# Attention, routing and a three-of-sixteen mixture of experts on one core: the two sums are filled in the attention's turns, and TensorE gets unread products at two joints

## The reference, cut to what matters

```
x: (4, 1024, 256) f32
proj = x @ W_in.T + b_in                    # q, k, v: 16 heads of 64
q, k = rope(q), rope(k)
att  = softmax(causal(q @ k.T / 8))
x    = layernorm(x + (att @ v) @ W_out.T + b_out)
gates = softmax(x @ gate)                   # 16 experts
top 3 of the 16 per token, their gates scaled to a sum of 1
y    = sum over the 3 chosen e of gate_e * (relu(x @ W1[e] + b1[e]) @ W2[e] + b2[e])   # hidden 512
out  = layernorm(x + y)
```

## Time and profile before

| What | Value |
| --- | --- |
| median of 3 runs | 1839.72 us (1834.96 to 1841.53) |
| profiled execution, its own time | 1837.63 us |
| span of its trace | 1834.3 us |
| busy, share of the span | PE 92%, DVE 75%, POOL 67%, ACT 39% |
| attention | 0 to about 1284 us |
| routing | about 1285 to 1360 us |
| experts | about 1360 to 1794 us |
| last phase | about 1794 to 1834 us |

### The profile page before, as it was taken

The page is one execution under the profiler, slowest core; times in us unless marked ns, Lnnn a source line. Parts: engine busy times, 40 slices in busy tenths (PEclk is TensorE's granted clock), DMA queues, the critical chain, the costliest instruction groups (busy, mean ns, idle before and its releaser), DMA issues. The chain is left out here.

```text
span 1834.3 us, 34020 instructions
## 1 busy us (share of the span) xinstructions
PE 1686.4 (92%) x9515; PEld 1264.3 (69%) x9516; DVE 1383.9 (75%) x3235; ACT 722.0 (39%) x1519; POOL 1233.9 (67%) x1064
## 2 busy tenths in 40 slices
PE   4689999999999999999999999998659999999990
PEld 3556667666766677666766676664339999999980
DVE  3578888888888888988888898875776566656654
ACT  2234444444445544444444444543332222222222
POOL 3256788677877777788767787764017777777764
PEclk8799999999999999999999999999759999999995
DMA  9976556655665676456666565542974444444448
GB/s 307 336 207 162 154 168 199 182 164 157 184 163 156 209 205 179 140 160 187 199 188 187 166 188 142 161 127 98 355 241 72 71 73 74 71 73 74 71 65 278
DMA packets 185058, 302.36 MB, mean 165 GB/s; under 512 B 23120, under 2 KB 82384, under 8 KB 184800
## 3 DMA queue, kind: packets, MB, share of 16 engines
q1 hardware_dynamic: 161360, 269.20, 49.7%
q0 software_dynamic: 21504, 30.29, 10.4%
q10 hardware_dynamic: 2064, 1.31, 0.3%
HBM read 188.81 MB, written 111.67 MB: 164 GB/s over the span
## 5 line engine op out<-in xcount | busy, mean ns | idle before, releaser
L780 ACT ACTIVATE prob<-b_ps 128x512 f32<-128x512 f32 (+3 forms) x768 | 354.4, 488 | 360.3 <-PE b_ps L589 260.3
L516 POOL TENSOR_TENSOR acc<-acc,prob 128x1024 f32<-128x1024 f32 (+1 forms) x192 | 352.8, 1837 | 6.4 <-POOL acc L516 3.6
L588 PE MATMUL b_ps<-q,k 128*128 128x512 f32 (+3 forms) x768 | 296.1, 390 | 5.3 <-ACT prob L780 3.5
L489 POOL TENSOR_TENSOR roped<-rot 128x512 f32<-128x512 f32 x128 | 174.5, 1364 | 165.0 <-DVE rot L919 164.2
L581 PE MATMUL a_ps<-k,q 128*128 128x512 f32 (+3 forms) x768 | 265.8, 383 | 20.5 <-DMA k<-scratch_hilo 10.1
L670 PE MATMUL y_ps<-prob,v_sb 128*64 128x512 f32 (+3 forms) x1536 | 272.9, 490 | 0.1
L899 DVE CUSTOM_DVE_ANT_0 masked<-a_ps,causal 128x128 bf16<-128x128 f32 (+3 forms) x512 | 237.3, 479 | 45.9 <-PE a_ps L581 37.7
L589 PE MATMUL b_ps<-q,k 65*128 65x512 f32 (+3 forms) x768 | 264.4, 348 | 0.0
L1449 POOL DMA_INDIRECT scratch_sum<-y,dst_i x112 | 187.6, 1675 | 94.8 <-ACT y L1521 90.9
L948 DVE RECIPROCAL inv<-inv 128x128 f32<-128x128 f32 x256 | 232.2, 929 | 7.7 <-ACT inv L821 5.3
L494 POOL TENSOR_TENSOR lo<-roped,hi 128x512 fp32r<-128x512 f32 x128 | 176.8, 1382 | 80.6 <-ACT hi L793 80.6
(11 more groups left out here) (255 smaller groups left out, 2382.9 us busy)
## 6 DMA issues: line engine op xcount, KB each, us to landing
q<-scratch_hilo SPq DMA_DIRECT2D x192, 256.0 KB, 4.6
k<-scratch_hilo SPq DMA_DIRECT2D x192, 256.0 KB, 5.2
scratch_hilo<-hi SPq DMA_DIRECT2D x64, 512.0 KB, 3.8
scratch_hilo<-lo SPq DMA_DIRECT2D x64, 512.0 KB, 4.5
w_sb<-scratch_wsplit SPq DMA_DIRECT2D x32, 512.0 KB, 3.6
w<-in_L_ffn_W_dram SPq DMA_DIRECT2D x32, 512.0 KB, 9.9
wv_sb<-scratch_wsplit SPq DMA_DIRECT2D x16, 512.0 KB, 5.9
xT<-scratch_xsplit SPq DMA_DIRECT2D x6, 1024.0 KB, 6.2
```

The costliest lines, as they stand in the source:

```text
L516: nc.gpsimd.tensor_tensor(sums, old, probs(q), ALU.add).then_inc(m["sum_p"], 1)
L588: nc.tensor.matmul(out, k1[s][:, h, js], q1[s][:, h, qs], start=True, stop=False, skip_group_check=True)
L780: nc.scalar.activation(probs(q)[:, h, :], b_ps[:, h, 0:w], ACT.Exp).then_inc(exp_done[h], 1)
```

## The change

Three edits. First, SP writes 24 tiles of `sum0` right behind the same tile's store to `xn`, in the turns 14, 22 and 30, and `sum1` in 11 pieces of 3 tiles at the end of the turns 12 to 22; what is left in the routing phase is the last quarter of `sum0`, and the wait for all sums ahead of the biases is gone. Second, PE executes products of the identity with itself that nobody reads (`keep_warm`): 26 ahead of the counting products, 12 behind the last one-hot batch, at the end of the routing phase. Third, 10 more at the start of the expert phase.

```
+def keep_warm(nc, out, ident, count):
+    for _ in range(count):
+        nc.tensor.matmul(out, ident[:], ident[:], start=True, stop=True, skip_group_check=True)
...
+ZEROS_FROM, ZERO_PIECES = 12, 11
+ZERO_TILES = (TILES + 1) // ZERO_PIECES
...
+            first_sum = dram["sum0"].rearrange("(t p) d -> p t d", p=P)
+            zeros = shared["vo"][:].rearrange("p (t d) -> p t d", t=1)
+            def put_zeros(i, first, end):
+                rows = dram[f"sum{i}"].rearrange("(t p) d -> p t d", p=P)[:, first:end, :]
+                sp.dma_start(rows, zeros.broadcast_to([P, end - first, D])).then_inc(shared["sums_in"], 16)
...
                     sp.dma_start(xn[b][:, i, :], rows).then_inc(m["x_st"], 16)
+                    sp.dma_start(first_sum[:, TB * b + i, :], rows).then_inc(m["x_st"], 16)
                 if place == LN_STORE + 1 and b < B - 2:
-                    sp.wait_ge(m["x_st"], 16 * (TB * b + i + 1))
+                    sp.wait_ge(m["x_st"], 32 * (TB * b + i + 1))
...
+                if ZEROS_FROM <= it < ZEROS_FROM + ZERO_PIECES:
+                    sp.wait_ge(m["zeroed"], 1)
+                    put_zeros(1, ZERO_TILES * (it - ZEROS_FROM), ZERO_TILES * (it - ZEROS_FROM + 1))
...
-            sp.wait_ge(m["zeroed"], 1)
-            sp.wait_ge(m["o_done"], 4 * (STEPS - 1))
-            zeros = shared["vo"][:].rearrange("p (t d) -> p t d", t=1)
-            for i in range(SUMS):
-                rows = dram[f"sum{i}"].rearrange("(t p) d -> p t d", p=P)[:, TILES if i == 0 else 0:TILES + 1, :]
-                sp.dma_start(rows, zeros.broadcast_to([P, rows.shape[1], D])).then_inc(shared["sums_in"], 16)
-            sp.wait_ge(m["x_st"], 16 * TB * (B - 1))
+            put_zeros(0, TILES, TILES + 1)
+            sp.wait_ge(m["x_st"], 32 * TB * (B - 1))
...
+            sp.wait_ge(m["r_x1"], LG)
             first = dram["sum0"].rearrange("(t p) d -> p t d", p=P)
-            for b in range(2):
-                sp.wait_ge(x1_in[b], 16)
-                sp.dma_start(first[:, b * TB:(b + 1) * TB, :], S["x1a"][:, b * TB:(b + 1) * TB, :]).then_inc(S["sums_in"], 16)
-            sp.wait_ge(m["r_x1"], LG)
-            sp.dma_start(first[:, 2 * TB:4 * TB, :], S["x1b"][:]).then_inc(S["sums_in"], 16)
+            sp.dma_start(first[:, 3 * TB:4 * TB, :], S["x1b"][:, TB:2 * TB, :]).then_inc(S["sums_in"], 16)
             sp.wait_ge(m["r_xtr"], UNITS_DONE - FIRST)
-            sp.wait_ge(S["sums_in"], 16 * (SUMS + 3))
...
+            keep_warm(nc, all_ps[:, 0:P], ident, 26)
             pe.wait_ge(m["r_mask"], GROUPS)
...
                 if a == 2:
                     count_begun()
+            keep_warm(nc, all_ps[:, 0:P], ident, 12)
...
-            pool.wait_ge(S["sums_in"], 16 * (SUMS + 3))
+            pool.wait_ge(S["sums_in"], 16 * (ZERO_PIECES + 2))
...
+            keep_warm(nc, yo_ps[:, 0, 0:P], ident, 10)
             turn_x(0, 0)
             turn_x(1, 1)
```

## The result

| | median | runs | ratio to before, 95% interval |
| --- | --- | --- | --- |
| before | 1839.2 us (1833.46 to 1843.18) | 18 | |
| with the change | 1844.89 us (1839.82 to 1848.91) | 18 | 1.0027 (1.0019 to 1.0036) |

The change makes the kernel slower by 0.27%, 5.0 us (3.5 to 6.6). The prediction was 1841.2 us, +1.5, "within 0.5%": the time lies in its range and within 0.5% of before, but the loss is about three times the sum, and the time lies 1.9 us above the forecast's own narrower range (1839.5 to 1843). The profiled execution took 1845.57 us, 7.9 more than the one before; its span, 1843.5, is 9.2 longer.

What follows compares the result with a forecast made beforehand. TensorE was taken to bound attention and experts, so only about 1312 to 1372 us could move the end: 0 + 0.8 + 1.6 - 0.9 = +1.5, 1841.2 us. Own range 1839.5 to 1843; 8 in 10, 1835.5 to 1846.

Steps and rivals of the forecast that it cites:

- the zero taken for the sums: Attention and routing: moving the sums' writes changes nothing, 0 us, since PE's waits show room.
- The fourth rival: Attention, SP's turns 12 to 30: added stores delay ScalarE's row of maxima, PE waits; +12.6 us, 1855 in all, chance 0.05.
- The sign that the prediction named: Attention: the prediction is wrong if PE's waits there gain transfers of more than 2 us in sum.
- The counts, +0.8 taken: Routing, 26 products ahead of the counts: overshoot the mask by 1.8 us, counts gain from full clock; +0.8 us.
- the upper end, +1.7: Routing counts: operand read with a stride might gain nothing from the clock, 0.90 us each; +1.7 us.
- The block's end, +1.6 taken: Routing's end, 12 products: PE's DRAIN stands behind them and comes last; +1.6 us, range +1.2 to +2.1.
- The third rival: Routing block's end doesn't wait for unread products: -1.4 us, 1838.3, chance 0.05.
- The experts' start, -0.9 taken: Experts' start, 10 products during the first gathers: faster clock for the first layers, between -2.2 and 0; -0.9 us.
- the first rival: Routing to experts: no rise in the twelve, fall before first layers, counts without gain; +4.1 us, 1843.8, chance 0.15.
- the wide range: Whole kernel: the 8 in 10 range, 1835.5 to 1846 us, taking in three rivals and the runs' spread.

Runs made afterwards that it cites:

- the kernel with all parts together: Moved sums, 10 products at the experts' start, SP's turn 30 held until ScalarE's row landed, mask contiguous, against the kernel before: 0.9969, median 1835.51 us.

## Why the prediction was right, and where it was short

**Where the kernel can lose.** That the windows of the attention would not move was right (PE is busy 1093.11 us from 100 to 1200, before 1092.33), and the zero taken for the sums holds within 2 us (1.0000, 0.9989 to 1.0012). The fourth rival's place was real, but the stores that the change adds are not its cause; the transfers that were there before are enough. In the eleven traces in which turn 30 isn't held back, PE's wait there was, in the seven with single stores, 0.9, 2.2, 1.1, 3.0, 1.6, 0.8 and 1.1 us, mean 1.5, and in the four with doubled ones 2.1, 1.0, 1.7 and 0.8, mean 1.4. The two spread alike. The sign that the prediction named, more than 2 us of new waits for transfers in the attention, did not come: at the row of maxima it was +1.2.

**The counts, +0.8 taken, +1.87 measured.** The mechanism (26 overshoot the pause by 1.8 us) was right; the step that failed is "at full clock I take 0.45 each". It had the right doubt beside it, the stride, and the upper end, +1.7, for it. The rows held a hint that was not weighed: 0.90 us for 512 columns, when the one-hot products of 112 columns, read without a stride, take 0.53 for four (448 columns) at the same clock.

**The block's end, +1.6 taken, 1.9, 1.4 and 1.5 measured.** Right, and the DRAIN was the right row: it lasts as long as the products queued ahead of it. The clock rose in the twelve, 3.8 to 5.1 us after their start, in the changed kernel's first trace only 0.3 us before their end. The third rival is out. The Trainium skill's queue of 64 instructions ("TensorE: Matmul & The Clock Gate", the table at its head) may hold, no run here shows its depth; but the block's end doesn't go by it: the DRAIN of 3.92 us disagrees with any reading in which unread products are free.

**The experts' start, -0.9 taken, about -0.5 measured.** B is 17.11, 16.13 and 16.78 in the three traces with 12 and 10, mean 16.7; the eight traces with neither have 14.26 to 16.26, mean 15.5. So the two together lose 1.1, as a difference of means: the smallest of the three lies inside the spread of the eight. With a mean slip of 1.6 that leaves a gain of 0.5, not 0.9. With the 10 and without the 12, B is 14.00 and 13.95. The loss sits in the order: the 12 bring the clock up too early. The prediction had seen that the clock might fall there again.

**Sum.** 1.9 + 1.1 = +3.0 us, against +1.5 forecast; the 1.9 repeats to 0.01 us in all three traces with the 26. The two series of the change gave +5.0 (3.5 to 6.6) and +2.8 (-0.2 to 5.7). What is between 3.0 and 5.0 is not settled; no stage of the traces shows it, the interval of the moved sums alone would hide 2 us, and a longer series would be needed to tell it from chance. So the measured time came nearest to the first rival (1843.8, chance 0.15), and of its three conditions two came true, the counts without gain and the fall at the first layers; the third, no rise in the twelve, came only near to it. That the time lies in the wide range owes something to the spread of the runs, which was taken into it: the forecast's own range missed.

## What to carry to other kernels

Unread products are not free at a block's end, nor ahead of a wait that they can outlast: count their time at the slow clock, and let them end when the real work comes, neither later nor much before. Before paying for a faster clock, read off whether the operation follows the clock at all; a product with a strided operand didn't. A transfer that is covered by work in every turn of a pipeline may be bare in the last turns, where that work has run out; here PE's waits for the row of maxima stood there.

## What the runs showed of the hardware that was not expected

A pause of PE can cost more than its length. In turn 30 the clock fell in all five traces with a wait from 1.6 to 3.0 us for the row, and in none of the six with 0.8 to 1.1. From one row of maxima to the next it took 16.0 to 16.4 us without a fall, and 18.5 to 21.3 with one: 2 to 5 us more, for 1 or 2 more of waiting. The wait alone does not decide it: the kernel with all parts together had none, only the pause of 1.26 us for DVE that the kernel before has too (1.25), and its clock fell behind it. How much of the 12 us by which runs of one and the same kernel differ comes from such falls is not shown: the slowest profiled execution, 1846.74 us with the 26 alone, had no fall in turn 30, but a mean clock of 0.70 from 1284 to 1312, where the other traces have 0.82 to 0.94.

A product of 512 columns of bf16 read with a stride of 16 elements starts its successor after 0.89 to 0.90 us at either level of the clock, and after 0.40 us at 1.2 GHz without the stride (two traces). DVE writing 128 elements of bf16 with a stride of 32 took 0.71 us instead of 0.29.
